# A graph attention layer on one core: one head's messages on GpSimd instead of two, and the table of sources transposed four tile pairs later

## The reference

```
Q, K, V = x @ Wq, x @ Wk, x @ Wv                   # (6250, 8, 64) each
score = exp(clip(sum_d(K[src] * Q[dst]) / 8, -5, 5))   # one per edge and head
wV = segment_sum(V[src] * score, dst)              # the messages, added up per node
Z  = segment_sum(score, dst)
h  = x + wV / (Z + 1e-6)
y  = (h - mean(h)) * rsqrt(var(h) + 1e-5) * gamma + beta   # over the nodes
out = layernorm(x + y)                              # over the features
```

## Time and profile before

| | |
|---|---|
| median of 3 runs | 2132.28 us (2130.37 to 2133.13) |
| the profiled execution, its own time | 2120.94 us |
| its span in the trace | 2119.0 us |
| PE busy | 2000.0 us (94%) |
| DVE busy | 1798.0 us (85%) |
| ACT busy | 1387.7 us (65%) |
| POOL busy | 1345.6 us (63%) |
| HBM, read and written | 289 GB/s over the span |

### The profile page before, as it was taken

One profiled execution on the slowest core, in us unless ns is written; L12 is line 12 of the kernel. 1 busy time (PEld: TensorE's weight loads), 2 busy tenths in 40 slices (PEclk: granted clock), 3 DMA queues, 4 the chain that ended last, 5 costly groups with the idle time before them and its releaser, 6 DMA issues. The chain is left out here.

```text
span 2119.0 us, 42794 instructions
## 1 busy us (share of the span) xinstructions
PE 2000.0 (94%) x8139; PEld 1364.6 (64%) x8140; DVE 1798.0 (85%) x2536; ACT 1387.7 (65%) x4649; POOL 1345.6 (63%) x1612
## 2 busy tenths in 40 slices
PE   8998999987999999999999999999999999998998
PEld 4555555545777777776777777776777777774343
DVE  6678555546999999999999999999999999998968
ACT  0000000005888888888888888888888888888745
POOL 0104344346888888888888888888888888881000
PEclk9999999997999999999999999999999999999999
DMA  5646666768999998899998999989999999996234
GB/s 182 176 128 220 233 238 232 234 199 318 319 321 316 329 329 316 316 325 321 332 324 310 326 328 324 323 319 316 329 330 320 310 329 324 326 316 219 72 104 174
DMA packets 184221, 588.34 MB, mean 278 GB/s; under 512 B 28688, under 2 KB 30448, under 8 KB 184176
## 3 DMA queue, kind: packets, MB, share of 16 engines
q0 software_dynamic: 135904, 465.14, 62.1%
q1 hardware_dynamic: 44752, 120.87, 16.6%
q10 hardware_dynamic: 3520, 1.81, 0.4%
HBM read 534.48 MB, written 78.91 MB: 289 GB/s over the span
## 5 line engine op out<-in xcount | busy, mean ns | idle before, releaser
L629 POOL DMA_INDIRECT kv<-kv_d,idx x880 | 908.3, 1032 | 231.4 <-issue 221.9
L792 PE MATMUL acc<-kv,mm_sb 128*128 128x260 f32 x3520 | 873.9, 392 | 43.2 <-POOL kv L596 27.2
L704 ACT ACTIVATE kv<-kv 128x64 f32<-128x64 f32 x3520 | 888.8, 334 | 14.3
L792 PEld LDWEIGHTS acc<-kv,mm_sb 128*128 128x128 f32 x3520 | 644.1, 190 | 227.6 <-issue 137.9
L667 DVE TENSOR_TENSOR kv<-q_ps,kv 128x1024 f32<-128x1024 f32 x440 | 538.1, 1223 | 76.4 <-PE q_ps L771 48.6
L771 PE MATMUL q_ps<-q_tile,mm_sb 128*128 x1760 | 551.9, 435 | 30.5 <-issue 21.3
L674 DVE TENSOR_REDUCE raw<-kv 128x16 f32<-128x1024 f32 x440 | 532.4, 1210 | 0.0
L771 PEld LDWEIGHTS q_ps<-q_tile,mm_sb 128*128 128x128 f32 x1760 | 324.9, 190 | 136.3 <-issue 85.0
L596 POOL TENSOR_TENSOR kv<-kv 128x256 f32<-128x256 f32 x440 | 279.6, 636 | 16.9 <-ACT kv L718 9.2
L714 ACT ACTIVATE mm_sb<-mm_ps,less 128x1024 fp32r<-128x1024 f32 x220 | 241.2, 1097 | 23.6 <-issue 14.5
L596 DVE TENSOR_TENSOR kv<-kv 128x256 f32<-128x256 f32 x440 | 207.6, 472 | 8.3 <-ACT kv L718 7.5
(11 more groups left out here) (138 smaller groups left out, 1451.4 us busy)
## 6 DMA issues: line engine op xcount, KB each, us to landing
q_tile<-q_d SPq DMA_DIRECT2D x49, 512.0 KB
x_res<-xb_d SPq DMA_DIRECT2D x56, 256.0 KB, 5.4
kv<-kv_d,idx POOLq DMA_INDIRECT x880
q_d<-q_a SPq DMA_DIRECT2D x25, 512.0 KB, 2.7
kv_d<-kv_a SPq DMA_DIRECT2D x25, 512.0 KB
xb<-in_x POOLq DMA_DIRECT2D x49, 256.0 KB, 3.7
xb_d<-xb POOLq DMA_DIRECT2D x49, 256.0 KB, 2.7
out_rows<-agg SPq DMA_DIRECT2D x49, 256.0 KB, 2.0
```

What stands on the lines that cost most here:

```text
L629: pool.indirect_dma_start(kv[:, s, u, 0:2 * DIM], None, kv_d, bass.IndirectOffsetOnAxis(idx[:, s, u:u + 1], 0), bounds_check=N_NODES - 1, ...
L704: return act.activation(v, v, ACT.Copy, scale=kv[:, s, u, 2 * DIM + h:2 * DIM + h + 1])
L792: last = pe.matmul(acc[:, bass.ds(par, 1), DIM - (1 - n) * HALF:DIM + n * HALF], m, kv[:, sc, u, DIM + n * HALF:DIM + (n + 1) * HALF], sta ...
```

## The change

POOL_HEADS goes from 2 to 1. In `attend`, POOL's `weigh` now covers head 7 alone, 128x128 elements instead of 128x256, and DVE's `weigh` covers heads 4 to 6, HEADS - ACT_HEADS - POOL_HEADS = 3 heads, 128x384 instead of 128x256. The number of instructions and all semaphores stay.

TABLE_DUO goes from 8 to 12. PE's seven transposes (L307), its waits for s_visit, s_c22 and s_trc there, and DVE's wait for s_tr and copy (L476) move from tile pair 8 to tile pair 12.

```
-POOL_HEADS = 2
+POOL_HEADS = 1
...
-        TABLE_DUO = 8
+        TABLE_DUO = 12
```

## The result

The changed kernel took 2171.11 us (median of 4 runs, 2166.93 to 2174.07) beside 2131.32 for the kernel before on the same chip: ratio 1.0189, 95% interval 1.0164 to 1.0214. It was timed twice more, on two different chips (which chip the first timing had isn't on record). There it took 2125.43 beside 2125.52 us (ratio 0.9995, 0.9985 to 1.0005) and 2122.00 beside 2124.41 us (0.9991, 0.9979 to 1.0004). So the forecast gain of 92 us isn't there on any occasion; on two of three nothing changed, and on one 40 us were lost. I call the three the first, second and third timing. The profile shown here is that of the first; its own time is 2172.05 us, its span 2170.1.

A forecast was written before the change was run, and what follows sets the result against it. POOL was taken to set the attention stage's pace; 3.262 to 3.06 us a pair gives 86 us, plus 6 us in the projections, 92 us in all: 2040 us. Own range 2012 to 2067, 8 in 10: 2004 to 2096.

The forecast's parts named there:

- What bounds the kernel before: Attention stage: POOL, back to back for 3.19 of 3.262 us a pair, sets the pace; DVE and PE follow closely.
- (a): POOL's message in attention: 128 columns cost about 0.31 us, saving 0.32 us a pair, nearly proportional to columns.
- (b): DVE's message in attention: 384 columns instead of 256 add 0.13 us, making DVE's unblocked cycle 2.95 us.
- (c): Blocking between POOL and DVE in attention: POOL's shorter message met less often, DVE's longer L596 more; 0 to 0.24 us.
- rival 1: Attention: POOL-DVE blocking stays and all comes onto the path, 3.19 us a pair, 2095 us; chance 0.16.
- rival 4: Attention: POOL and DVE lock in each pair, 3.62 us a pair, slower at 2280 us; chance 0.05.
- rival 5: Attention: POOL isn't the pacer, or one 0.31 us collision a pair takes the gain; only projections gain 6 us; chance 0.03.
- (d): Friction of closely matched engines in attention: 2% on the highest floor of 3.00, giving 3.06 us a pair, gain 86 us.
- (e): DMA in attention: same bytes in less time, 343 GB/s, within reach since 411 was seen; no cost.
- Rival 3: Attention: DMA bounds, engines at 95% with today's packet times, 3.13 us a pair, 2070 us; chance 0.06.
- Rival 2: Attention: little friction, the stage runs about at the floors, 2.98 us a pair, 2003 us; chance 0.10.
- (f): Projections: moving the table to tile pair 12 removes a stall, costs 0.8 us there; gain 6 us, between 4.7 and 9.4.

The follow-up runs named there:

- e10: The kernel before with only the coarse half of the queries multiplied (two L771 matmuls a pair instead of four): 2115.56 us, ratio 0.9958.
- e13: The changed kernel with a slot given back in two halves, the first gather waiting only for L792's first-tile products: 2135.79 us, ratio 1.0044 to the kernel before.
- e3: The changed kernel with POOL_LAG = 5 instead of 6, so POOL makes its messages one pair earlier: 2141.96 us, ratio 1.0081 to the kernel before.
- e14: The kernel before with a slot given back in two halves, the first gather waiting only for L792's first-tile products: 2117.78 us, ratio 0.9965.
- e18: The changed kernel with PE's one-hot matrices block (L774 to L782, every second step) moved behind L792: 2135.57 us, ratio 1.0069 to the kernel before.
- e12: The changed kernel gathering 896 of 1024 columns, head 7's sources set to zero once: 2126.78 us, ratio 1.0012 to the kernel before.
- e2: The kernel before with TABLE_DUO = 12 alone: 2121.01 us, ratio 0.9986.
- e15: The changed kernel with POOL's loop over the rounds written out and a slot given back in two halves: 2118.35 us, ratio 0.9959 to the kernel before.
- e11: The changed kernel with POOL_LAG = 5 and only the coarse half of the queries multiplied: 2095.89 us, ratio 0.9870 to the kernel before.

## Why the prediction was wrong

**What bounds the kernel before: right, as far as it went.** POOL is back to back there (173 ns of idle time before a pair's gathers, where 160 is the usual gap), and e10 fits it: with half of L771 left out, the kernel before gained only 0.4%.

**(a) POOL's message: mis-sized.** 413 to 415 ns, not 310. The saving is 0.22 us a pair and not 0.32; the cost isn't proportional to the columns down to 128.

**(b) DVE's message: right.** 552 to 560 ns, where 420 + 130 = 550 was forecast.

**(c) Blocking: right in direction, and rivals 1, 4 and the collision of rival 5 fall by rows.** L677 fell from 360 to 214 ns and L596 shows no stretch, so what is left is about 0.05 us a pair. The rule of the Trainium skill (SBUF — State Buffer, section Who interferes with whom) gives 3.26 us if one takes a full collision in each pair. The second timing's pair does take 3.27 us, but these rows have no such collision: a rule can name the right time for a wrong reason.

**(d) Friction: this is the step that failed.** I took 2% on the highest engine's floor of 3.00 us, that is 0.06 us a pair, from the excess that the kernel before has over its pacer. The measured excess is 0.27 us (3.27) and 0.37 in the first timing (3.374). The 2% was that of a stage in which one engine never waits, and the others' waits hide behind it. The step that it left out is POOL's own wait for a free slot: it was named in (d) ("the gathers wait for the segment matmuls of eight pairs earlier") and priced only within the 2%. What the runs showed in its place: as soon as POOL's message is of one head, POOL's idle time before a pair's gathers rises from 0.17 to 0.34 us (0.50 in the first timing) and its gathers take 0.06 us longer (0.01 in the first), which is the whole saving of 0.22 us and more. The slot's turn was not added up either. With the smallest waits that the traces show (0.29 to L792, 0.84 to the gather), the shortest pair of gathers (2.32) and the mean L792 and message (1.98, 0.47), it needs 5.90 us for two pairs, 2.95 a pair: as near as PE, DVE and POOL. In the kernel before the gather came 1.09 us after L792's end on average, 0.25 over the smallest, while POOL was still at its message: there was little left to take.

**What is shown and what is argued.** Shown: the gain of POOL's message comes back as POOL's idle time behind late signals and as longer gathers, as its records add up; relief of one of TensorE, DVE, the transfers' bytes or the slot's release alone gives 0.4% or less, and some reliefs lose; lag 5 and half the query products together give 1.3% though one alone loses. It is argued, not shown, that two turns of nearly equal length hold the stage, the slot's (message, L792, gather, message) and the queries' (L667, L771, L667, with one buffer q_ps and L792 on PE between), and that what shortens one lets PE's order lengthen the other. The late signals are a rival to that: they stall POOL behind its own second gather, and an earlier release (e13) or an earlier message (e3) doesn't remove them. No run removed them from the changed kernel, so what the pair would take without them isn't known. **Open:** why POOL's waits end late in the changed kernel, and why more so in the first timing. The late signals are rare where POOL's message is of two heads (4% in before, 0% in e10, 6% in e14) and make up 23 to 52% in the table where it is of one; e18 shows that which pairs have them depends in part on the one-hot matmuls ahead of L792, but its time didn't fall. No run here brought the first timing's rhythm back, so what sets it off wasn't found.

**(e) DMA: right.** No bound; e12 shows it with 12.5% fewer bytes and the same time. Rival 3 falls. That 343 GB/s is within reach wasn't tested: the changed kernel never moved more than 322 in the stretch. Rival 2 falls by the time alone.

**(f) The table: the mechanism was right and the size off.** The stall left tile pair 8, pair 12 pays its 0.8 us and has none, and DVE is late next in pairs 7 to 9, as said. The prediction's upper bound had one misreading: PE's wait of 2.26 us for L345 ends at 206.48, behind the second tile pair's end (199.84), and belongs to the third. First L667: 5.05 us earlier in the first timing, 3.6 in the second, 2.2 in the third. Over all runs it stands at 478.09 us in the 13 profiles with the table at 12 and at 480.91 in the 7 with it at 8: 2.8 us, and e2 measures 0.14%, 3 us. The forecast was 6, with 4.7 as lower bound. The first timing's tile pair 7 took 19.4 us; in 6 of the 13 profiles with the table at 12 it took 21.1 to 21.4. Why isn't known.

**Expectations of what would show it.** L677 well under 360, DVE's 550 and the gathers' waits for L792 came as said. 310 ns, 3.06 us, DVE over 97% busy (89%) and 343 GB/s (312) did not. I had listed the gathers' waits for L792 as a sign of being right; they showed that the gain was going, and L792's end didn't set them.

**A version that beats both.** With the whole computation, e15 (change, released in halves, loop written out, 0.9959), e14 (before, released in halves, 0.9965) and e4 (change, loop written out, 0.9971) are the best, 0.3 to 0.4% each, and their intervals overlap. e11, at 0.9870, leaves out the low part of the queries.

## What to carry to other kernels

When engines and rings of buffers lie within 10% of each other, add up each turn that passes through several engines (who frees the slot, who waits for that, how long from the release to the first instruction that uses it), and put its floor beside the engines' floors. An engine with no wait in its row is the pacer, but its excess over its own work says nothing about the friction once it waits too. When a profile puts a wait down to another engine, compare the waiter's time with that engine's recorded end: if they move apart, as in e3 and e13, look for the cause at the waiter. If work is taken from one member and the time stays, try two reliefs together before more of one. And time a loss again on another chip before explaining it.

## What I hadn't expected of the hardware

- POOL's multiply of two SBUF operands takes 413 ns at 128 columns, 636 at 256 and 1302 at 512. An estimate from the first two and from the copy of 8 columns (200 ns): about 0.2 us stay however short it is.
- A gather that waits starts 0.83 us (825 to 830 ns in most cases) after the signal it waited for, 0.76 with the loop written out. The same work is hidden while POOL has a message of 0.62 us to do, and no longer when it has one of 0.41.
- A signal of TensorE for which POOL waits can stand 0.2 to 0.9 us behind the recorded end of its last matmul at lag 6 (431 ns on average in the first timing, 14 in e10) and up to 2.7 at lag 5, while the records of the matmuls behind it start as usual. Signals of DVE, ACT and POOL mostly stand 8 to 12 ns behind their ends. The late ones keep their distance to POOL's second gather and not to the matmul. The trace doesn't say what on POOL holds them.
- The same program differed by 2% between occasions (2171 and 2125 us) while the kernel before differed by 0.3% (2131 and 2125).
